# Linear attention's last head group normalised from a transposed reciprocal, and layer-norm statistics moved to the end of the projection

## What is computed

```python
xn = layernorm(x)
q, k, v = xn @ Wq.T, xn @ Wk.T, xn @ Wv.T        # 16 heads of 16
q, k = taylor_feature_map(q), taylor_feature_map(k)
kv = cumsum(k[..., None, :] * v[..., :, None])   # over the rows, causal
y = einsum(q, kv)
denom = sum(q * cumsum(k)) + EPS
attn = (y / denom) @ Wo.T
```

## Time and profile before

| | us |
|---|---|
| median of three runs | 3475.45 (3474.73 to 3481.47) |
| time of the profiled execution | 3475.38 |
| its span | 3473.6 |
| first part, from the span's start to the second part's first hT load | 873.9 |
| TensorE busy over the span | 3330.0 (96%) |
| VectorE busy over the span | 2736.3 (79%) |

### The profile page before, as it was taken

One profiled execution on the slowest core, in us unless ns is written; L12 is line 12 of the kernel. 1 busy time (PEld: TensorE's weight loads), 2 busy tenths in 40 slices (PEclk: granted clock), 3 DMA queues, 4 the chain that ended last, 5 costly groups with the idle time before them and its releaser, 6 DMA issues.

```text
span 3473.6 us, 96643 instructions
## 1 busy us (share of the span) xinstructions
PE 3330.0 (96%) x36960; PEld 2498.5 (72%) x36960; DVE 2736.3 (79%) x8256; ACT 2518.9 (73%) x5629; POOL 1536.3 (44%) x1547
## 2 busy tenths in 40 slices
PE   7898889887799999999999999999999999999999
PEld 4555545554588787788788788888788888888887
DVE  4767777777688888888888888888888888888886
ACT  5667776666577777777777777777777777777775
POOL 4444444444444444444444444444444444444443
PEclk9999999999899999999999999999999999999999
DMA  6756676654422222222222222222222222222211
GB/s 159 174 128 139 126 154 144 141 100 87 134 63 62 73 66 62 73 67 62 73 66 62 73 67 62 73 66 62 73 68 62 72 67 62 72 69 62 71 45 43
DMA packets 289965, 293.94 MB, mean 85 GB/s; under 512 B 40960, under 2 KB 221536, under 8 KB 288992
## 3 DMA queue, kind: packets, MB, share of 16 engines
q1 hardware_dynamic: 289504, 287.74, 34.7%
HBM read 104.89 MB, written 58.73 MB: 47 GB/s over the span
## 4 chain that ended last, share of the span: by engine, by line
PE 73%; DVE 1%; POOL 0%; ACT 0%; issue 0%; DMA 0%; SPq 0%; DVEq 0%; POOLq 0%
PE f_ps L1575 19%; PE f_ps L1683 16%; PE f_ps L1695 10%; PE f_ps L1660 6%; PE f_ps L1639 4%; PE f_ps L1580 3%; PE f_ps L1602 3%; PE f_ps L1620 3%; PE f_ps L1649 2%; PE f_ps L1609 2%; PE f_ps L1688 2%; PE f_ps L1624 2%; PE f_ps L1667 1%; PE f_ps L1561 0%; ACT pr L1491 0%
## 5 line engine op out<-in xcount | busy, mean ns | idle before, releaser
L1246 POOL TENSOR_TENSOR turned<-qk,rot 128x256 f32<-128x256 f32 x512 | 405.4, 813 | 1250.5 <-ACT qk L1458 1235.4
L1575 PE MATMUL f_ps<-wqkv_s,hT 128*128 128x512 f32 x1536 | 707.2, 596 | 8.9 <-DMA hT<-xnT_dram 5.5
L1683 PEld LDWEIGHTS f_ps<-hnT,w_s 128*128 128x128 f32 x5120 | 591.7, 192 | 63.0 <-issue 59.8
L1326 DVE CUSTOM_DVE_ANT_0 pr<-f_ps,masks_s 128x192 f32<-128x192 f32 x1024 | 326.4, 355 | 360.7 <-PE f_ps L1609 358.7
L1683 PE MATMUL f_ps<-hnT,w_s 128*128 128x128 f32 x5120 | 592.5, 275 | 2.5 <-DVE hnT L1383 2.5
L1491 ACT ACTIVATE pr<-pr,nmax,rnorm 128x192 f32<-128x192 f32 x1024 | 545.0, 535 | 44.4 <-DVE nmax L1333 44.4
L1575 PEld LDWEIGHTS f_ps<-wqkv_s,hT 128*128 128x128 f32 x1536 | 276.9, 191 | 273.6 <-issue 186.7
L1343 DVE TENSOR_SCALAR pr<-pr,rsum 128x192 f32<-128x192 f32 x1024 | 445.4, 497 | 9.0
L1695 PE MATMUL f_ps<-w_s,act_u 128*128 128x256 f32 x1536 | 352.7, 379 | 0.0
L687 ACT ACTIVATE weights<-t_ps,four_s 128x1024 f32<-128x1024 f32 x320 | 326.4, 1132 | 26.1 <-PE t_ps L843 26.1
L1253 POOL TENSOR_TENSOR rnorm<-ssq,f_mhalf 128x8 f32<-128x8 f32 x128 | 255.7, 1998 | 163.9 <-DVE ssq L1303 163.9
(11 more groups left out here) (151 smaller groups left out, 6873.5 us busy)
## 6 DMA issues: line engine op xcount, KB each, us to landing
vw<-vw SPq DMA_DIRECT2D x628, 128.0 KB, 2.5
qkT<-parts_dram SPq DMA_DIRECT2D x384, 128.0 KB, 5.7
kT<-kT SPq DMA_DIRECT2D x124, 256.0 KB, 2.7
parts_dram<-shared SPq DMA_DIRECT2D x64, 384.0 KB, 3.1
xnT_dram<-xnT SPq DMA_DIRECT2D x8, 1025.0 KB, 5.4
xs<-x_dram SPq DMA_DIRECT2D x8, 1024.0 KB, 7.4
xn_dram<-xn SPq DMA_DIRECT2D x8, 1024.0 KB, 5.0
attn_dram<-ao SPq DMA_DIRECT2D x8, 1024.0 KB, 9.6
```

Source lines behind the costliest of these rows:

```text
L1246: g.tensor_tensor(turned[:, heads, f], qk[:, heads, z], sines, ALU.mult).then_inc(done, 1)
L1326: last = v.tensor_tensor_reduce(out=chances(h), in0=ps[:, SCORES[p], k * 256:k * 256 + BAND], in1=mask_of(it)[:, HALF - k * HALF:HALF - k ...
L1575: last = mm(ps[:, b, :], rows, wqkv_s[:, l, c, i * INNER:(i + 1) * INNER], start=(c == 0), stop=(c == KC - 1))
L1683: last = mm(ps[:, UP[j // 2], o:o + P], w1_s[:, l, c, half * FULL + j * P:half * FULL + j * P + P], hnT[:, c, :], start=(c == 0), stop=(c ...
```

## The change

Four edits, all in `taylor_block`:

- Group 3's denominators take the way of the others: `read_den(b, 3)` (the transfer into `den_flat`), `invert_den`, `write_den(b, 3)` and `spread_den`, a full 128x1024. There is no `keep_den` for it; VectorE's `normalise(b, t)` keeps its last two instructions (L422, L425) and loses its shuffle and its reciprocal.
- VectorE's `project` is reordered around this; two blocks of the fourth to eighth are no longer behind a normalised tile.
- The statistics of batch b+2 (`tile_stats` of 8 tiles and `variances`) are taken at the end of `project(b + 1, b)` and no longer in groups 0 and 1; GpSimd's `root` moves ahead of its first `pairs`.
- `layer_norm` writes two tiles in every group, 0 to 3, and none behind the last.

```diff
-            def invert(b, g):
+            def read_den(b, g):
                 sp.wait_ge(yT_ready, 2 * (b * GROUPS + g) + 2)
+                sp.dma_start(den_flat[:, :], yT[ONE[g % 2]:P:VP, g, :]).then_inc(den_in, 16)
+            def write_den(b, g):
+                sp.wait_ge(den_inverse, b * GROUPS + g + 1)
                 if g >= 1:
-                    sp.wait_ge(y_group, i)
+                    sp.wait_ge(y_group, b * (GROUPS - 1) + g)
+                elif b >= 1:
+                    sp.wait_ge(y_ready, b * TILES)
...
                 for g in range(GROUPS - 1):
                     if g + 2 < GROUPS:
                         load_heads(b, g + 2)
-                    invert(b, g)
+                    read_den(b, g)
+                    write_den(b, g)
+                read_den(b, GROUPS - 1)
                 if b + 1 < B:
                     store_xn(b + 1)
                 if b + 2 < B:
                     load(b + 2)
+                write_den(b, GROUPS - 1)
                 if b + 1 < B:
                     heads(b + 1)
                 store_attn(b)
...
             def attention(b):
+                if b + 1 < B:
+                    root(b + 1)
                 pairs(b, 0)
                 pairs(b, 1)
-                if b + 1 < B:
-                    root(b + 1)
                 pairs(b, 2)
...
                 if t == 0:
-                    dve.wait_ge(yT_ready, 2 * (b * GROUPS + GROUPS))
                     dve.wait_ge(y_group, b * (GROUPS - 1) + g)
-                else:
-                    dve.wait_ge(y_tile, i)
-                v.stream_shuffle(den[:, cols], yT[:, g, cols], [ONE[odd]] * 32).then_inc(den_ready, 1)
-                dve.wait_ge(den_ready, i + 1)
-                v.reciprocal(den[:, cols], den[:, cols]).then_inc(rden_ready, 1)
-                dve.wait_ge(rden_ready, i + 1)
+                    dve.wait_ge(spread, SPREADS * (b + 1))
                 v.scalar_tensor_tensor(yT[:, g, cols], yT[:, g, cols], keep_s[:, odd:odd + 1], den[:, cols], ALU.mult, ALU.mult)\
                     .then_inc(y_tile, 1)
...
             def project(b, last=None):
                 if last is not None:
-                    for t in range(3):
-                        normalise(last, t)
-                for m in range(BLOCKS // 2):
+                    invert_den(last, GROUPS - 1)
+                for m in range(2):
+                    subtract_high(b, m)
+                if last is not None:
+                    spread_den(last, GROUPS - 1)
+                for m in range(2, BLOCKS // 2):
                     subtract_high(b, m)
                 dve.wait_ge(xnT_ready, b * TILES + TILES)
                 v.reduce_sum(xsum[:, :, :], xnT[:, :, 1:].rearrange("p c (t n) -> p c t n", n=P), AX).then_inc(xsum_ready, 1)
                 if last is not None:
-                    normalise(last, 3)
+                    for t in range(3):
+                        normalise(last, t)
                 for m in range(BLOCKS // 2, BLOCKS):
+                    subtract_high(b, m)
                     if last is not None:
-                        normalise(last, m)
-                    subtract_high(b, m)
+                        normalise(last, m - 1)
+                if last is not None:
+                    normalise(last, TILES - 1)
+                if b + 1 < B:
+                    for t in range(TILES):
+                        tile_stats(b + 1, t)
+                    variances(b + 1)
...
                     mask_diagonals(g, 1)
-                    if following is not None and g <= 1:
-                        for t in range(4 * g, 4 * g + 2):
-                            tile_stats(following, t)
-                    if following is not None and g >= 2:
-                        layer_norm(following, 2 * (g - 2))
-                        layer_norm(following, 2 * (g - 2) + 1)
+                    if following is not None:
+                        layer_norm(following, 2 * g)
+                        layer_norm(following, 2 * g + 1)
                     if g >= 2:
                         spread_den(b, g - 2)
                     mask_diagonals(g, 2)
-                    if following is not None and g <= 1:
-                        for t in range(4 * g + 2, 4 * g + 4):
-                            tile_stats(following, t)
-                    if following is not None and g == 1:
-                        variances(following)
...
                 add_before(GROUPS - 1, 1)
-                if following is not None:
-                    for t in range(TILES // 2, TILES):
-                        layer_norm(following, t)
                 spread_den(b, GROUPS - 2)
                 keep_den(b, GROUPS - 2)
...
             attention(B - 1, None)
+            invert_den(B - 1, GROUPS - 1)
+            spread_den(B - 1, GROUPS - 1)
             for t in range(TILES):
                 normalise(B - 1, t)
```

More of the change, by code:

```diff
@@ L165, in taylor_block @@
         y_pair = sem("y_pair")
-        den_ready = sem("den_ready")
-        rden_ready = sem("rden_ready")
         y_tile = sem("y_tile")
@@ L181, in taylor_block @@
         PIECE = SEQ // 4
+        SPREADS = 2 * (GROUPS - 1) + 1
         UNITS = [(kind, i, pair) for kind, i, pair in
@@ L218, in load @@
                 sp.dma_start(xs[:, :, :], x[b].rearrange("(t p) d -> p t d", p=P)).then_inc(x_in, 16)
-            def invert(b, g):
-                i, row = b * (GROUPS - 1) + g, ONE[g % 2]
+            def read_den(b, g):
                 sp.wait_ge(yT_ready, 2 * (b * GROUPS + g) + 2)
-                sp.dma_start(den_flat[:, :], yT[row:P:VP, g, :]).then_inc(den_in, 16)
-                sp.wait_ge(den_inverse, i + 1)
+                sp.dma_start(den_flat[:, :], yT[ONE[g % 2]:P:VP, g, :]).then_inc(den_in, 16)
+            def write_den(b, g):
+                sp.wait_ge(den_inverse, b * GROUPS + g + 1)
                 if g >= 1:
-                    sp.wait_ge(y_group, i)
-                sp.dma_start(den[row:P:VP, :], den_flat[:, :]).then_inc(den_out, 16)
+                    sp.wait_ge(y_group, b * (GROUPS - 1) + g)
+                elif b >= 1:
+                    sp.wait_ge(y_ready, b * TILES)
+                sp.dma_start(den[ONE[g % 2]:P:VP, :], den_flat[:, :]).then_inc(den_out, 16)
             def store_xn(b):
@@ L321, in normalise @@
             def normalise(b, n):
-                pool.wait_ge(spread, 2 * (b * (GROUPS - 1) + n) + 2)
+                pool.wait_ge(spread, SPREADS * b + 2 * n + 2)
                 for c in range(0, SEQ, PIECE):
@@ L394, in invert_den @@
             def invert_den(b, g):
-                dve.wait_ge(den_in, 16 * (b * (GROUPS - 1) + g + 1))
+                dve.wait_ge(den_in, 16 * (b * GROUPS + g + 1))
                 v.reciprocal(den_flat[:, :], den_flat[:, :]).then_inc(den_inverse, 1)
             def spread_den(b, g):
-                dve.wait_ge(den_out, 16 * (b * (GROUPS - 1) + g + 1))
+                dve.wait_ge(den_out, 16 * (b * GROUPS + g + 1))
                 v.stream_shuffle(den[:, :], den[:, :], [ONE[g % 2]] * 32).then_inc(spread, 1)
             def keep_den(b, g):
-                dve.wait_ge(spread, 2 * (b * (GROUPS - 1) + g) + 1)
+                dve.wait_ge(spread, SPREADS * b + 2 * g + 1)
                 v.tensor_scalar_mul(den[:, :], den[:, :], keep_s[:, g % 2:g % 2 + 1]).then_inc(spread, 1)
```

## The result

The changed kernel takes 3526.09 us in the median of four runs (3524.7 to 3531.7), against 3475.09 us of the kernel before beside it. The ratio is 1.0149, with a 95% interval of 1.0131 to 1.0168: slower by 51 us, where 53 us were forecast. The profiled execution took 3526.99 us (span 3525.2).

A forecast was written before the change was run, and what follows sets the result against it. The prediction took nearly gapless TensorE to bound the changed first part (busy 753 of 873 us). Terms -4.9 - 2.8 - 0.6 + 54 + 7 = +52.7 on 3475.38 gave 3528 us; own range 3510 to 3546.

The forecast's parts named there:

- The moved wait, +54: Attentions 1 to 6, group 0: VectorE's layer_norm waits for the attention output's store, delaying TensorE's state; six times 9.0 us.
- The median landing and not the fast one: The output's store was taken to land 9.6 us after issue; rival landing at 4.6 us gives 3498, chance 0.08.
- The clock, +7: Behind each of six waits, TensorE's idling takes the granted clock to half: 1.2 us each, between nothing and 2.
- The projections, -4.9: Seven projections: TensorE's wait before the values of tile 6 falls from 1.58 to 0.88 us, 0.7 us each.
- the wait falls to that: 0.7 us: With less normalisation ahead of the first subtraction, TensorE's wait before tile 6's values falls from 1.58 to 0.88 us.
- The last batch, -2.8: End of the last batch: transfer of 3.2 us, one shuffle, faster tiles; ScalarE's last copy at 869.8 against 872.56.
- Statistics and root at nothing, and -0.6 in attention 0: Statistics fit VectorE's idle 6.66 us, root free; one pair fewer in group 0 saves 0.6 us in attention 0.
- The range: The forecast's own range was 3510 to 3546: landings of 8 to 11 us and the bounds of the clock.

The follow-up runs named there:

- split_stored: The changed kernel with a semaphore of its own for xn's stores, so layer_norm no longer waits for the attention output's store: 3471.09 us, ratio 0.9987.
- norm_late: The changed kernel with layer_norm back at its old places (groups 2, 3 and behind the last), statistics still at the projection's end: 3469.19 us, 0.9984.
- store_early: The changed kernel with the attention output's store issued ahead of the 12 loads of group 1's heads, the wait untouched: 3487.69 us, 1.0037.
- constant_first: The changed kernel with the load of the second part's constant issued ahead of the output's store, the wait untouched: 3546.76 us, 1.0201.
- split_four: split_stored with four tiles of the last group, not three, normalised ahead of the fifth subtraction: 3467.44 us, 0.9975.
- denominators_four: denominators_only with four tiles of the last group, not three, normalised ahead of the fifth subtraction: 3465.72 us, 0.9972.
- denominators_only: The kernel before with only the fourth group's denominators through the transfers and the new order in project; statistics, root and layer norm unmoved: 3466.89 us, 0.9975.
- statistics_only: The kernel before with only the moves of statistics, root and layer norm; the fourth group stays on VectorE tile by tile: 3531.74 us, 1.0162.

## Why the prediction was right

The time, 3526.1 us, is 2 us from the 3528 forecast, and the mechanism is the one named. The agreement to 2 us owes something to luck: against the forecast, the projections gave 3.4 us less and attention 7 took 2.5 more, while the clock took 4.2 less and the last batch gave 1.2 more. The terms one by one:

- *The moved wait, +54.* Right in place, number and size. Six waits of VectorE, 9.4 us each (56.4 in all), the state 53.5 us later in sum. Inside the term small errors cancel too. The landing was taken as 9.6 and was 10.1 in the mean of the six; but the store was issued 0.4 us earlier behind the attention's start than before the change (5.5 and 5.9 in the mean), and the way from landing to state was 3.97 and not 4.1. split_stored, norm_late, store_early and constant_first show it from four sides.
- *The median landing and not the fast one.* Right: with the 12 loads ahead the store took 10.1 us in the median, without them 5.7 (store_early). By the estimate from the Trainium skill ("DMA: Bandwidth & Descriptors", section "Anatomy of one DMA") it would be 4.4 us. The section has measured its fit on DMAs issued from GpSimd, and this store is issued by SyncE. The runs come near it only at the last batch's 4.6 us, with nothing ahead; at 5.7 us without the loads and 10.1 behind them the measurement decides.
- *The clock, +7.* Right in kind, too large in size. Attentions 1 to 6 lost 56.3 us, of which 53.5 up to the state; so what came behind is +2.8 in sum, and that includes other waits, which differ from attention to attention by more than a microsecond. The clock did fall to half in the stretch behind the wait.
- *The projections, -4.9.* The step "the wait falls to that: 0.7 us" held: the waits before the values of tile 6 are 7.0 us in eight, 0.9 each. What failed is that they are kept. Normalising tile 6 behind the last subtraction makes a new wait, and 0.5 of each 0.7 us are given back; -1.5 in all. split_four and denominators_four get the 0.7 us in full. That the shorter normalisation gives the 0.7 us is right (denominators_only), but it is not the only way there: in statistics_only the normalisation is as long as before, and the move of layer norm gives the same 0.7.
- *The last batch, -2.8.* -4.0. The term mis-sized is the transfer, taken as 3.2 us and landed after 1.92.
- *Statistics and root at nothing, and -0.6 in attention 0.* The statistics cost nothing that can be told (norm_late). The -0.6 did not come, the state is at 11.57 us there against 11.47. There each tile of layer norm takes 0.86 us and not the 0.48 of the earlier trace rows, beside GpSimd: two of them take what four tiles of statistics took before (0.41 us each). The root delays the pairs by some 2 us and not 1: in batch 2 they start 3.8 us behind the attention's start, not 1.8. Together with layer norm in group 0 this costs 0.6 us at the state once the big wait is gone (split_stored, 11.24 against 10.66).
- *Attention 7, +2.5.* In no term. TensorE waits there 1.6 us for a load of heads and 1.0 us for nothing the profile shows, which it did not before. Whether the change makes these or only shifts them was not tested. The length of this attention varies much: in the ten experiments it is 62.9 to 67.5 us, though the state comes at 9.9 to 10.3 us in all of them.
- *The range.* Its upper end, 3546, is what landings of 11.7 us and 2 us for the clock give; with the 11 us that the prediction names it would be 3541.

## What to carry to other kernels

When work is moved earlier in an engine's order, its waits move too: for each, look up which event it counts, who issues that event and what stands ahead of it in that queue. A semaphore shared by several kinds of transfer makes a wait ask for more than its data need; one for each kind cost nothing here and gave back 55 us. And after a stall has been removed from an engine's order, look at what is now last in it: 0.5 of 0.7 us went back to the one tile that had been put behind the last subtraction.

## What the runs showed of the hardware that was not expected

- VectorE's small SBUF operations beside GpSimd's can take three to four times as long: 1.26 us and not 0.34, 1.13 us and not 0.29, for 128x128. In the changed kernel the multiplications of tiles 5 and 6 and the addition of tile 6 are the slow ones in all seven projections; the last batch, with GpSimd idle, has none. The forecast took the medians of these lines for every tile.
- A transfer of 16 KB into `den` landed 1.92 us after its issue on an idle queue.
- TensorE paused 2.76 us in attention 1 of the kernel before and 5.96 us in store_early, in the middle of one `attend`, for which the profile shows no releaser. Both pauses end within some 2 us of the fall of the DMA share from about 1 (0.96 and 1.04) to 0.22 and 0.16, behind the issue of a 3 MB load. The traces show more: the first parts of the twelve profiles have 62 such pauses of over 1 us, and every one ends 1.2 to 1.7 us after a 16 KB packet of the DMA queue that the profile calls "instruction" has ended (there are 79 such packets in some 900 us). In store_early that packet runs from 186.46 to 188.01, and TensorE goes on at 189.34. So TensorE seems to wait there for its own instructions. No run changed this, so it stays an inference.
